# Gate stages of a graph-and-expert kernel rebuilt: bias rows per item, counts in five products, rows by one-hot products, tiles one by one

## The reference

```python
gates = softmax(x @ Wg + bg)                        # first mixture: 8 experts, hidden 1536
topg, topi = top_k(gates, 2); topg = topg / sum(topg)
y[e] = gelu(x @ W1[e] + b1[e]) @ W2[e] + b2[e]      # only the chosen experts matter
out = sum over the two choices of topg * y[chosen]

top = argmax(x @ Wg + bg)                           # second mixture: 4 experts, hidden 384
out = gelu(x @ W1[top] + b1[top]) @ W2[top] + b2[top]
```

## Time and profile before

| what | value |
|---|---|
| median of 3 runs | 1471.71 us (1467.08 to 1474.52) |
| profiled execution, its own time | 1465.52 us |
| its span | 1463.0 us |
| TensorE busy | 1287.5 us, 88% |
| VectorE busy | 920.1 us, 63% |
| ScalarE busy | 560.8 us, 38% |
| GpSimd busy | 127.4 us, 9% |
| mean granted TensorE clock | 0.931 of full speed |

### The profile page before, as it was taken

One profiled execution on the slowest core, in us unless ns is written; L12 is line 12 of the kernel. 1 busy time (PEld: TensorE's weight loads), 2 busy tenths in 40 slices (PEclk: granted clock), 3 DMA queues, 4 the chain that ended last, 5 costly groups with the idle time before them and its releaser, 6 DMA issues.

```text
span 1463.0 us, 18209 instructions
## 1 busy us (share of the span) xinstructions
PE 1287.5 (88%) x6567; PEld 1088.3 (74%) x6567; DVE 920.1 (63%) x1748; ACT 560.8 (38%) x981; POOL 127.4 (9%) x114
## 2 busy tenths in 40 slices
PE   5999999999999899986788999999966687967786
PEld 3677489799699766566588999999955587946543
DVE  4477655554644655546459999999965798244213
ACT  2111313413512333450058888888831364010010
POOL 0000200000000000110200000000060563010101
PEclk9999999999999999997599999999987889976699
DMA  9320462203105200313258999999961000010276
GB/s 334 133 86 29 173 216 108 98 1 141 65 1 216 87 1 1 113 40 130 86 216 295 370 379 377 385 371 373 355 225 51 25 1 1 0 65 1 97 253 209
DMA packets 81778, 223.46 MB, mean 153 GB/s; under 512 B 4972, under 2 KB 18348, under 8 KB 81592
## 3 DMA queue, kind: packets, MB, share of 16 engines
q1 hardware_dynamic: 75256, 192.79, 36.1%
q0 software_dynamic: 6464, 29.89, 5.6%
HBM read 195.92 MB, written 26.74 MB: 152 GB/s over the span
## 4 chain that ended last, share of the span: by engine, by line
PE 71%; DVE 16%; DMA 5%; issue 3%; ACT 2%; POOL 2%; ACTq 0%; SPq 0%; DVEq 0%; POOLq 0%
PE dve_ps L720 10%; PE dve_ps L721 10%; PE dve_ps L722 10%; PE dve_ps L763 4%; PE act_ps L720 3%; PE act_ps L721 3%; PE act_ps L722 3%; PE dve_ps L809 3%; DMA slot<-in_e1w 2%; PE act_ps L936 2%; PE dve_ps L953 2%; PE act_ps L760 2%; DVE part_slot L2041 2%; PE dve_ps L1175 2%; DVE part_slot L2032 2%
## 5 line engine op out<-in xcount | busy, mean ns | idle before, releaser
L2032 DVE TENSOR_TENSOR part_slot<-slot,item_hi 128x768 fp32r<-128x768 f32 x156 | 137.7, 951 | 0.9 <-ACT item_hi L1499 0.8
L1499 ACT ACTIVATE item_hi<-slot 128x768 fp32r<-128x768 f32 x156 | 118.0, 838 | 34.2 <-DMA slot<-in_e0w 31.5
L2041 DVE TENSOR_TENSOR part_slot<-slot,item_hi 128x768 fp32r<-128x768 f32 x132 | 116.5, 952 | 0.0
L720 PE MATMUL act_ps<-item_hi,hid_hi 128*128 128x384 f32 x288 | 98.8, 343 | 4.8 <-DVE hid_lo L2209 4.8
L1507 ACT ACTIVATE item_hi<-slot 128x768 fp32r<-128x768 f32 x132 | 100.0, 877 | 7.0 <-DMA slot<-in_e0w 6.8
L720 PE MATMUL dve_ps<-item_hi,x_hi 128*128 128x384 f32 x288 | 98.3, 341 | 2.9 <-DVE part_slot L2032 1.7
L721 PE MATMUL act_ps<-part_slot,hid_hi 128*128 128x384 f32 x288 | 99.0, 344 | 0.0
L722 PE MATMUL act_ps<-item_hi,hid_lo 128*128 128x384 f32 x288 | 97.7, 339 | 0.0
L721 PE MATMUL dve_ps<-part_slot,x_hi 128*128 128x384 f32 x288 | 97.2, 337 | 0.0
L722 PE MATMUL dve_ps<-item_hi,x_lo 128*128 128x384 f32 x288 | 96.9, 337 | 0.0
L1390 ACT ACTIVATE h_t<-act_ps,par 128x256 f32<-128x256 f32 x36 | 21.1, 587 | 122.4 <-PE act_ps L827 122.4
(11 more groups left out here) (395 smaller groups left out, 3254.6 us busy)
## 6 DMA issues: line engine op xcount, KB each, us to landing
slot<-in_e0w SPq DMA_DIRECT2D x48, 2304.0 KB, 10.3
slot<-in_w SPq DMA_DIRECT2D x9, 2304.0 KB, 9.6
slot<-in_e1w SPq DMA_DIRECT2D x12, 1152.0 KB, 6.2
ea_raw<-in_edge SPq DMA_DIRECT2D x8, 1024.0 KB, 5.4
slot<-in_wqkv SPq DMA_DIRECT2D x3, 2304.0 KB, 15.2
item_x<-xs SPq DMA_DIRECT2D x17, 384.0 KB, 9.7
xs<-zrow POOLq DMA_DIRECT2D x2, 3072.0 KB, 15.7
ys<-item_y POOLq DMA_DIRECT2D x16, 384.0 KB, 6.3
```

The costliest lines, as they stand in the source:

```text
L720: mm(to, kept[0], moved[0], start=start, stop=False)
L1499: go(item_hi[j][k][:, :], slot[s][:, k * D:(k + 1) * D], ACT.Copy).then_inc(up_high[j], 1)
L2032: vv.tensor_tensor(part_slot[s][:, ks], slot[s][:, ks], item_hi[j][k][:, :].bitcast(F32), ALU.subtract).then_inc(up_low[j], 1)
L2041: vv.tensor_tensor(part_slot[s][:, ks], slot[s][:, ks], item_hi[j][k][:, :].bitcast(F32), ALU.subtract).then_inc(down_low[j], 1)
```

## The change

The two gate stages are written anew. The stages `xt1`, `gate0`, `bias0`, `xt3`, `gate1` and `bias1` go.

- *Bias rows.* The eight products with `b2` and the additions to `xres` go, and with them the turned gate. POOL loads the `b2` row of each item's expert, spread over all 128 partitions, into `b2row` (`load_b2`), the first ahead of everything, each later one behind the store of the item before. `result` adds the row instead of copying, and waits for it.
- *Counts.* One product with `tri` over the four tiles' `sel` and a column block of zeros, and four with `ones` over ever fewer columns, all summed in one bank (`rank_tokens`).
- *Rows of items 0 and 1.* `pick_rows` multiplies one-hot matrices with the high and the low parts of the normalised rows, 16 single-pass products of 384 columns each. The result comes out in rows, ScalarE copies it to `item_x` (`keep_rows`), and `turn_x` transposes it. Item 0's one-hot matrix needs only counts and `sel` of expert 0, so it is made ahead of the plan; item 1's (`second_rows`) is made behind it. Item 1 is no longer read from DRAM. In run 0, item 1's row product stands between the two halves of item 0's up product.
- *Tiles one by one.* Each tile is turned, copied and given its logits by itself. In gate stage 0, `rescale` runs for tiles 0 and 1, then 2, then 3; in gate stage 1 for each tile. ScalarE makes the high parts of the normalised rows (`gate_tiles`), DVE the low parts (`low_rows`).
- *Moved.* DVE makes the low parts of the first half of item 0's up weights ahead of the attention output; those of the second half are made on POOL. `share_last` stands behind item 1's `x_in`. SP asks for the next up weights without waiting for the scatters in between.

The diff, cut to its core:

```diff
--- before
+++ after
...
-    ("xt1", 3, 3), ("gate0", 0, 3), ("bias0", 0, 8),
     ("xt2", 3, 3), ("h1", 4, 4), ("mask", 0, 4), ("gat1", 0, GH * 3), ("o1t", 4, 4), ("h2", 4, 4),
-    ("gat2", 0, 9), ("xt3", 3, 3), ("gate1", 0, 3), ("bias1", 0, 8),
+    ("gat2", 0, 9),
...
-                    if j == 0:
-                        sp.wait_ge(run.scattered_in, 16 * NT * run.picks)
-                        load_x(1)
+                sp.wait_ge(run.scattered_in, 16 * NT * run.picks)
                 sp.wait_ge(x_turned, 4)
...
-                sp.wait_ge(run.scattered_in, 16 * NT * run.picks)
-                load_x(1)
...
-            def gates(run, xt, ne, stage, bias_stage, b2, k_in):
-
-                pe.wait_ge(*k_in)
-                bank = dve_bank(0, DVE0[stage])
-                for t in range(NT):
-                    for k in range(DC):
-                        last = mm(bank[:, t * ne:(t + 1) * ne], xt[:, k, t * P:(t + 1) * P], wg[:, k, 0:ne],
-                                  start=(k == 0), stop=(k == DC - 1))
...
-                for t in range(NT + 1):
-                    for m in range(min(t + 1, NT)):
-                        last = mm(bank[:, t * ne:(t + 1) * ne], tri[:, :] if m == t else ones[:, :], sel[:, m, 0:ne],
-                                  start=(m == 0), stop=(m == min(t, NT - 1)))
-                last.then_inc(sig.to_dve, 1)
...
-                pe.wait_ge(in_eb2, 16 if ne == NE0 else 32)
-                pe.wait_ge(sig.dve_freed, DVE0[bias_stage])
-                for u in range(8):
-                    t, half = u // 2, u % 2
-                    bank = dve_bank(u, DVE0[bias_stage])
-                    mm(bank[:, 0:HALF], gate_t[0:ne, t * P:(t + 1) * P], b2[:, half * HALF:(half + 1) * HALF],
-                       start=True, stop=True).then_inc(sig.to_dve, 1)
...
+            def turn_tile(run, t, source, before):
+
+                pe.wait_ge(normed, before + t + 1)
+                if t >= 2:
+                    pe.wait_ge(kept_act, 7 * run.layer + 2 * (t - 1))
+                for half in range(2):
+                    bank = act_ps[(2 * t + half) % RING]
+                    for j in range(3):
+                        c = 3 * half + j
+                        turned = nc.tensor.transpose(bank[:, j * P:(j + 1) * P], source[:, t, c * P:(c + 1) * P], ident[:, :])
+                    turned.then_inc(tile_turned, 1)
+
+            def tile_logits(run, t, xt):
+                if t < NT - 1:
+                    pe.wait_ge(kept_act, 7 * run.layer + 2 * (t + 1))
+                else:
+                    pe.wait_ge(kept_act, 7 * run.layer + 2 * NT - 1)
+                    pe.wait_ge(kept_dve, run.layer + 1)
+                ne = run.ne
+                for k in range(DC):
+                    last = mm(run.logit_bank[:, t * ne:(t + 1) * ne], xt[:, k, t * P:(t + 1) * P], wg[:, k, 0:ne],
+                              start=(k == 0), stop=(k == DC - 1))
+                if t == NT - 1:
+                    last.then_inc(logits_ready, 1)
+
...
+            def rank_tokens(run):
...
+                mm(run.count_bank[:, 0:(NT + 1) * ne], tri[:, :], sel[:, :, 0:ne], start=True, stop=False)
+                for t in range(1, NT + 1):
+                    last = mm(run.count_bank[:, t * ne:(NT + 1) * ne], ones[:, :], sel[:, 0:NT + 1 - t, 0:ne], start=False, stop=(t == NT))
+                last.then_inc(counts_ready, 1)
...
+            def pick_rows(run, i, highs, lows):
+
+                if i == 0:
+                    pe.wait_ge(rows_high, NT * (run.layer + 1))
+                    pe.wait_ge(rows_low, NT * (run.layer + 1))
+                    pe.wait_ge(kept_act, 7 * run.layer + 2 * NT - 1)
+                    pe.wait_ge(kept_dve, run.layer + 1)
+                else:
+                    pe.wait_ge(row_kept, 4 * run.layer + 2 * i)
+                pe.wait_ge(first_set[i], run.layer + 1)
+                for half in range(2):
+                    hs = slice(half * HALF, (half + 1) * HALF)
+                    for m in range(NT):
+                        for part in (highs, lows):
+                            picked = mm(run.pick_banks[half][:, 0:HALF], first_sel[i][:, m, :], part[m][:, hs],
+                                        start=(m == 0 and part is highs), stop=(m == NT - 1 and part is lows))
+                    picked.then_inc(picked_rows, 1)
...
+            for t in range(3):
+                turn_tile(run0, t, xn1, NT * (L + 1))
+            pe.wait_ge(in_gate, 48)
+            pe.wait_ge(sig.dve_freed, DVE0["wo"] + 5)
+            tile_logits(run0, 0, xn1_t)
+            turn_tile(run0, 3, xn1, NT * (L + 1))
+            for t in range(1, NT):
+                tile_logits(run0, t, xn1_t)
             pe.wait_ge(in_tri, 32)
-            gates(run0, xn1_t, NE0, "gate0", "bias0", e0b2_s, (in_gate, 48))
-
-            def stream_items(run, nodes_in):
...
-                def pick_x():
-
-                    pe.wait_ge(run.first_set, 1)
-                    for half, bank in enumerate(x_banks):
-                        for j in range(3):
-                            c = 3 * half + j
-                            for m in range(NT):
-                                picked = mm(bank[:, j * P:(j + 1) * P], nodes_in[:, m, c * P:(c + 1) * P], first_sel[:, m, :],
-                                            start=(m == 0), stop=(m == NT - 1))
...
+                pick_rows(run, 0, xn1_hi, xn1_lo)
+                turn_x(0)
+                times_up(0, (0,))
+                pick_rows(run, 1, xn1_hi, xn1_lo)
+                times_up(0, (1,))
                 turn_x(1)
+                pe.wait_ge(run.plan_set, 1)
...
+            for t in range(3):
+                weighted_sums(t)
+            turn_tile(run1, 0, xn3, NT * (L + 3))
+            turn_tile(run1, 1, xn3, NT * (L + 3))
+            weighted_sums(3)
+            turn_tile(run1, 2, xn3, NT * (L + 3))
+            pe.wait_ge(in_gate1, 16)
+            pe.wait_ge(sig.dve_freed, v0 + 6)
+            tile_logits(run1, 0, xn3_t)
+            tile_logits(run1, 1, xn3_t)
+            turn_tile(run1, 3, xn3, NT * (L + 3))
+            tile_logits(run1, 2, xn3_t)
+            tile_logits(run1, 3, xn3_t)
+            pe.wait_ge(sig.dve_freed, v0 + 9)
+            rank_tokens(run1)
+            run_items(run1)
...
+            def gate_tiles(run, source, xt, highs, before):
+
+                for t in range(NT):
+                    ts = slice(t * P, (t + 1) * P)
+                    for half in range(2 if t < NT - 1 else 1):
+                        act.wait_ge(tile_turned, 2 * NT * run.layer + 2 * t + half + 1)
+                        go(xt[:, 3 * half:3 * half + 3, ts],
+                           act_ps[(2 * t + half) % RING][:, 0:HALF].rearrange("p (c n) -> p c n", c=3), ACT.Copy).then_inc(kept_act, 1)
+                    act.wait_ge(normed, before + t + 1)
+                    go(highs[t][:, :], source[:, t, :], ACT.Copy).then_inc(rows_high, 1)
+
+            def keep_rows(run, i):
+                for half in range(2):
+                    act.wait_ge(picked_rows, 4 * run.layer + 2 * i + half + 1)
+                    go(item_x[:, half * HALF:(half + 1) * HALF], run.pick_banks[half][:, 0:HALF], ACT.Copy).then_inc(row_kept, 1)
+
...
+            low_up(0, 0)
+            for ts in ((0, 1), (2,), (3,)):
+                for t in ts:
+                    for half in range(2):
+                        add_to_x("wo", t, half)
+                    gate_rows(t, xres)
+                rescale(ts, xres, xn1)
+            keep_turned(run0, xn1_t)
+            for t in range(NT):
+                low_rows(run0, t, xn1, xn1_hi, xn1_lo)
...
+                for t in range(NT):
+                    last = vv.tensor_scalar(first_sel[0][:, t, :], slot_iota[:, :], count[:, t, 0:1], sel[:, t, 0:1], ALU.is_equal, ALU.mult)
+                    if t < NT - 1:
+                        then(last)
+                    else:
+                        last.then_inc(first_set[0], 1)
...
+            def second_rows(run, n):
+
+                then(vv.tensor_scalar(pos_last[:, 0:n, :], pos[:, 0:n, :], -float(P), None, ALU.add))
+                settle()
+                for j in range(n):
+                    for t in range(NT):
+                        if j == 0:
+                            last = vv.tensor_scalar(first_sel[1][:, t, :], slot_iota[:, :], pos_last[:, 0, t:t + 1], None, ALU.is_equal)
+                        else:
+                            last = vv.scalar_tensor_tensor(first_sel[1][:, t, :], slot_iota[:, :], pos_last[:, 1, t:t + 1],
+                                                           first_sel[1][:, t, :].bitcast(F32), ALU.is_equal, ALU.add)
...
-                share_last(run)
+                second_rows(run, 2)
+                shares()
+                last = dve.value_load(plan_i[0:1, 16:17], min_val=run.items_min - 1, max_val=run.items_max - 1)
                 for j in range(2):
                     hidden(0, j)
```

(13 more changed lines are left out.)

285 lines of the change are left out of this document (139 added, 146 removed).

## The result

| | median of its runs | lowest to highest | profiled execution: span, granted clock |
|---|---|---|---|
| before | 1469.39 us | 1465.86 to 1474.52 | 1463.0 us |
| changed | 1417.74 us | 1410.35 to 1420.65 | 1416.8 us, 0.941 |

The changed kernel takes 0.964 of the time before (95% interval 0.961 to 0.967): 51.7 us less by the medians, 46.2 us less by the two profiled spans. The forecast was 1424.4 us, in a range of 1409 to 1440.

A forecast was written before the change was run, and what follows sets the result against it. Prediction: TensorE, 88% busy, paces the loop, and serial gate stages delay everything behind them. Stage 0 -35.4, stage 1 -21.9, added item traffic +10 sum to -47.3 us: 1424.4 us from the 1471.7 median, range 1409 to 1440.

The forecast's parts named there:

- last tile normalised: Gate stage 0: low parts moved ahead of the tiles and to GpSimd, tiles in three batches; last tile ready 8.0 us earlier.
- to the logits: Gate stage 0, last tile to logits: 11.4 us becomes 6.8, near the middle of 5.1 (full clock) to 9.0 (half); -4.6.
- counts to the row product, bias products in it: Gate stage 0: plan leaves the path, 8.1 us becomes 1.3 (-6.8); bias products go (-10.6).
- row product and its parts: Gate stage 0: 16 single-pass products at half clock, 5.6 us, then copy, turning, high and low parts; 9.9 becomes 8.5, -1.4.
- first items, to the third item's first load: Run 0's start: second row product and share_last cancel against the removed wait for item 1's rows and its turning; 0 us.
- stage 1: last tile: Gate stage 1: going tile by tile makes the last tile normalised later, 1333.1 against 1329.5 us, +3.6.
- One sign of the prediction: Run 0: first weight load of item 1 issued at 702 to 705 us.
- What is added to the items: Bias-row traffic of 0.39 MB per item: +4 us in run 0, +4 in run 1, +1 at each run's end; together +10.
- DMA-bound items: Rival: bias rows make the item loop transfer-bound, period 28.2 us, total 1433.4 us; chance 0.15.
- The full clock: Rival: TensorE keeps full clock in the shortened gate stages, 13.4 us more saved, 1411 us; chance 0.10.
- The hand-overs: Rival: tile-by-tile waits between engines eat stage 0's overlap, item 0's first products at half clock; 18 us lost, 1443; chance 0.10.
- A bias row that stalls each item of run 0: Rival, slower than before: results wait for late-landing bias rows; at 32 us landing the kernel takes 1501 us; chance 0.03.

The follow-up runs named there:

- low_on_dve: Changed kernel with the six low parts of item 0's second up weights on VectorE instead of GpSimd: 1411.02 us, 0.9608 of the kernel before.
- bias_alone: Kernel before with only the bias part: no transposed gates, bias products and adds; each item's bias row loaded and added with its result: 1446.69 us, ratio 0.9841.
- shares_early: Changed kernel with the selection of the last item's rows (share_last) moved between item 0's two hidden copies: 1416.92 us, 0.9660 of the kernel before.
- no_later_bias: Changed kernel with the bias row loaded only for item 0 of each expert run, later items adding that same row: 1412.66 us, 0.9613 of the kernel before.
- rows_narrow: Changed kernel with every bias row but the first loaded into 16 partitions, not 128, waits and issues kept: 1412.35 us, 0.9628 of the kernel before.
- rows_twice: Changed kernel with every bias row but the first loaded twice, the result waiting for both: 1430.47 us, 0.9752 of the kernel before.
- logits_early: Changed kernel with gate stage 0's logits of tiles 1 and 2 issued before the last tile's transposes: 1412.99 us, 0.9617 of the kernel before.

## Why the prediction was right

By its own steps, each from one instant of the profile to the next, changed less before:

| step | forecast | measured | from |
|---|---|---|---|
| up to the first attention-output add | 0 | +2.5 | 654.85, 657.36 |
| last tile normalised | -8.0 | -5.5 | 26.9, 21.4 |
| to the logits | -4.6 | -2.3 | 11.4, 9.1 |
| counts | -4.0 | -3.9 | 6.25, 2.3 |
| counts to the row product, bias products in it | -17.4 | -18.0 | 19.5, 1.5 |
| row product and its parts | -1.4 | -1.3 | 9.2, 7.9 |
| stage 0, with +0.1 for logits to sel | -35.4 | -30.9 | 76.9, 45.9 |
| first items, to the third item's first load | 0 | +0.9 | 63.3, 64.2 |
| loop of run 0 to its last result | +4 | +2.4 | 288.0, 290.4 |
| run 0's end to the weighted sums | +1 | +0.9 | 215.4, 216.3 |
| stage 1: last tile | +3.6 | +3.2 | 31.1, 34.3 |
| stage 1: to the logits | -6.4 | -6.4 | 13.0, 6.6 |
| stage 1: to the row product | -18.9 | -19.0 | 24.4, 5.4 |
| stage 1: row product and parts | -1.9 | -2.0 | 9.1, 7.1 |
| run 1 to the end, the first up product in it | +6.7 | +2.2 | 87.1, 89.3 |
| sum | -47.3 | -46.2 | 1463.0, 1416.8 |

The mechanism was right: the heads are serial, and what they save moves all that follows. The sum is right within 1.1 us, but in part by luck: stage 0 gave 4.5 us less than forecast, the steps of the items took 5.3 less, and the 2.5 us ahead of the change are no part of it (that add stands at 651.2 to 657.4 us in the other profiles). By the medians the change gave 51.7 us, 4.4 more than forecast. The step between the runs is known no better than the 5 us by which it differs from profile to profile.

- *Last tile.* Mis-sized by 2.5 us, of which 2.3 is the wait of VectorE's small operations for GpSimd. The sum had priced GpSimd's six operations by their own time and taken them as hidden. They took 11.65 us and not 10.7, and low_on_dve shows what they do to the engine beside them.
- *To the logits.* The middle between half and full clock was the wrong choice. It was half throughout: 36 records in 7.7 us, the upper bound of 9.0.
- *Counts, bias products, counts to the row product* hold to 0.6 us in both stages. The -10.6 for the bias rows alone was low by 2.2; bias_alone has 12.8, with the turned gate. In the sum it did not matter, since that part stood in the term beside it.
- *Row product and the first items.* The row product ran at half for most of its length, as taken. One sign of the prediction failed: the first weight load of item 1 was asked for at 712.4 us and not at 702 to 705, since the first up product started 7.0 us late against the forecast (703.3 and 696.3) and the load came 9.15 us behind that start in place of 6.8, with the clock at half for its first 3 us. The sum had priced that product at full clock. Yet the second row product and `share_last` against the wait for item 1's rows cancelled to 0.9 us over all the first items. shares_early adds what the sum had not seen: ScalarE's chain stands beside VectorE's there, so moving `share_last` gives nothing.
- *Stage 1* is right to 0.4 us in each step, the tile by tile loss of 3.2 us among them; in the six profiles where the clock rose sooner in the sums that loss is 1.7 to 1.9. The +1.7 for an up product at half clock did not come: the clock rose in the row product, and the up product took 4.12 us, as at 1375.95 in the earlier trace rows.
- *What is added to the items.* The size between the two bounds was chosen, +4, and 2.4 came. The mechanism that no_later_bias, rows_narrow and rows_twice show is the landing time. The loop has a little slack, and each row eats some. In run 1 the share of one row, 1.05 us, is what one weight load shows (1.1 to 1.4 us), but once and not in about four periods; the rest of the +4 and the +1 at the end can't be told from what run 1 differs by between profiles.

The rivals: DMA-bound items would have made the period 28.2 us, and even two rows make it 27.9. The full clock came neither by itself nor when the gap was closed. The hand-overs cost stage 1 its 3.2 us; in stage 0 the last tile was late by GpSimd's 2.3 us and not by them. A bias row that stalls each item of run 0 was not seen: no result of run 0 waited for one.

## What to carry to other kernels

A step on the path is worth its whole chain: removing eight products also removed the turned gate and a copy, and the time moved nearly whole to the end because every transfer behind it is issued when work is done and not at a set time. An operation moved to an engine that idles has still to be priced by what it does to its neighbours: 11.7 us on GpSimd cost VectorE 2.3 us on the path, and putting it into an idle stretch of VectorE gave as much in the time as that and four other edits together. A small transfer added to a loop with full queues costs less than its bytes there; where a load that is waited for stands beside it, it costs about all of them. And a long wait at the end of a run, 6.7 us for a row here, has no price while another chain ends later: follow the chain before you name one. Last, compare a stretch over several profiles before you read a microsecond from two; here unchanged code differs by 5 us.

## What the hardware showed that was not expected

- VectorE operations on 128x2 elements from memory took 0.86 and 1.77 us beside GpSimd subtractions and 0.17 without, while adds from PSUM (1.15 us for two) and statistics (1.02) beside them kept their times.
- TensorE's clock fell to 0.50 at 676 us in the midst of products of 8 columns that kept the engine busy by its records (logits_early: 4.00 of 4.00 us from 676 to 680, 2.56 of 3.00 before). It rose again within runs of wider products: of 384 columns in the changed kernel (at 699.6 us, 4 us into the row product), of 128 columns in the kernel before (at 727.6 us, 5 us into `pick_x`). What the clock goes by, no run here tells.
- The transfers of the loop went up from 377 to 393 GB/s when more was asked of them, at a share of 1.00 to 1.02, and the landing of 2304 KB from 10.4 to 12.1 us. The Trainium skill (DMA: Bandwidth & Descriptors, Bandwidth) gives about 358 GB/s a core for when both cores of an HBM domain stream, and more for a core by itself; this kernel runs on one core, and the traces agree with the latter, over 180 us on end. The prediction had taken the 358 GB/s for this case and found the trace against it.
